# A selective scan with two states on 64 partitions each, and a residual added on TensorE

## What is computed

```python
xz = jnp.einsum('bld,ed->ble', seq, in_proj_w)            # u and z, 256 channels each
u = silu(conv(u) + conv_b)
dt, Bm, Cm = jnp.split(einsum(u, x_proj_w), [8, 24], axis=-1)
dt = softplus(einsum(dt, dt_proj_w) + dt_proj_b)
def step(h, inputs):                                      # 256 channels x 16 states
    h = jnp.exp(dt_t[:, :, None] * A) * h + (dt_t * u_t)[:, :, None] * B_t[:, None, :]
    y = jnp.einsum('bdn,bn->bd', h, C_t)
y = (y + u * D) * silu(z)
x = x + einsum(y, out_proj_w)
t = t + ffn(layernorm(t))
```

## Time and profile before

| | us |
|---|---|
| median of 3 runs | 1285.89 |
| lowest, highest | 1283.64, 1287.6 |
| the profiled execution, its time | 1284.42 |
| its span in the trace | 1282.6 |
| DVE busy in it | 1150.1 |
| POOL busy in it | 1106.9 |
| PE busy in it | 1072.5 |
| ACT busy in it | 819.0 |

### The profile page before, as it was taken

The page is one execution under the profiler, slowest core; times in us unless marked ns, Lnnn a source line. Parts: engine busy times, 40 slices in busy tenths (PEclk is TensorE's granted clock), DMA queues, the critical chain, the costliest instruction groups (busy, mean ns, idle before and its releaser), DMA issues.

```text
span 1282.6 us, 13041 instructions
## 1 busy us (share of the span) xinstructions
PE 1072.5 (84%) x3642; PEld 613.6 (48%) x3642; DVE 1150.1 (90%) x1341; ACT 819.0 (64%) x1532; POOL 1106.9 (86%) x747
## 2 busy tenths in 40 slices
PE   5678878888888887888888889888878878888797
PEld 4334545545545544544455455445445445454344
DVE  1299999999999999999999999999999999999782
ACT  2476766766666667757667666666667676576543
POOL 4199898898898898998988988988988989989663
PEclk8699998998998999999999989989999999998898
DMA  6222221221222312212222212222122132222561
GB/s 162 76 76 76 81 100 65 98 100 58 99 76 86 101 57 105 100 57 98 87 77 80 101 57 99 93 71 99 59 102 101 57 105 100 74 99 87 181 206 37
DMA packets 64538, 116.78 MB, mean 91 GB/s; under 512 B 34218, under 2 KB 47954, under 8 KB 64466
## 3 DMA queue, kind: packets, MB, share of 16 engines
q1 hardware_dynamic: 64466, 115.96, 26.9%
HBM read 108.47 MB, written 7.47 MB: 90 GB/s over the span
## 4 chain that ended last, share of the span: by engine, by line
POOL 27%; DVE 24%; issue 21%; PE 19%; ACT 7%; POOLq 0%; DMA 0%; DVEq 0%; SPq 0%; ACTq 0%
POOL SCAN L414 15%; DVE SCAN L984 15%; PE Yp L711 7%; POOL SCAN L426 6%; DVE SCAN L939 5%; PE PP L740 2%; PE PP L862 2%; PE PP L790 2%; PE PP L842 2%; POOL XN L451 2%; PE PP L835 1%; DVE GATES L968 1%; ACT SGZ L599 1%; POOL GATES L419 1%; POOL XN L442 1%
## 5 line engine op out<-in xcount | busy, mean ns | idle before, releaser
L984 DVE TENSOR_TENSOR_SCAN SCAN<-DA,CAR,SCAN 128x384 f32<-128x384 f32 x768 | 729.8, 1000 | 39.3 <-POOL SCAN L426 35.7
L414 POOL TENSOR_TENSOR SCAN<-SCAN,CS 128x768 f32<-128x768 f32 x384 | 692.3, 1817 | 23.1 <-DVE SCAN L984 18.9
L711 PE MATMUL Yp<-SCAN,IDENT 128*128 128x384 f32 x1536 | 592.6, 511 | 101.1 <-POOL SCAN L414 93.0
L491 ACT ACTIVATE DA<-UDT,A 128x384 f32<-128x384 f32 x768 | 441.6, 581 | 365.3 <-DVE SCAN L984 362.5
L711 PEld LDWEIGHTS Yp<-SCAN,IDENT 128*128 128x128 f32 x1536 | 288.8, 198 | 309.8 <-POOL SCAN L414 147.3
L939 DVE TENSOR_TENSOR SCAN<-UDT,BB 128x768 f32<-128x768 f32 x288 | 268.4, 932 | 11.1 <-PE BB L693 9.2
L426 POOL TENSOR_TENSOR SCAN<-UDT,BS 128x768 f32<-128x768 f32 x96 | 174.4, 1817 | 0.0
L862 PE MATMUL PP<-XN,WT 128*128 128x384 f32 x384 | 140.4, 501 | 0.0
L446 POOL TENSOR_TENSOR UDT<-UDT 128x768 f32<-128x768 f32 x24 | 43.5, 1811 | 69.9 <-DVE UDT L1068 69.9
L862 PEld LDWEIGHTS PP<-XN,WT 128*128 128x128 f32 x384 | 75.6, 199 | 56.7 <-issue 11.7
L693 PE MATMUL BB<-PT,SEL 96*128 96x384 bf16 x288 | 97.7, 340 | 4.1 <-DVE SCAN L939 4.1
(11 more groups left out here) (167 smaller groups left out, 1090.2 us busy)
## 6 DMA issues: line engine op xcount, KB each, us to landing
CS<-bc_rows SPq DMA_DIRECT2D x96, 768.0 KB, 4.1
BS<-bc_rows SPq DMA_DIRECT2D x24, 768.0 KB, 6.0
out<-XN SPq DMA_DIRECT2D x32, 192.0 KB, 2.5
X<-in_x SPq DMA_DIRECT2D x24, 192.0 KB, 3.5
X<-in_L_ffn_memory_tokens SPq DMA_DIRECT2D x16, 256.0 KB, 3.0
XN<-in_L_ffn_memory_tokens SPq DMA_DIRECT2D x16, 256.0 KB, 3.3
bc_rows<-XDT SPq DMA_DIRECT2D x24, 48.0 KB, 1.5
...
```

The lines of the kernel that those rows point to most:

```text
L414: pool.tensor_tensor(M[:, n1 % MRING], HB[:, n1 % HRING], over_halves(CS[:, n1 % CRING]), ALU.mult).then_inc(m_ready, 1)
L491: act.activation(DA[:, h, 0:T], DT[:, par, h], ACT.Exp, scale=A[:, h, n:n + 1])\
L711: last = pe.matmul(Yp[:, h, 0:T], IDENT[:, :], M[:, n3 % MRING, h], start=n3 == 0, stop=n3 == NS - 1)
L984: dve.tensor_tensor_scan(HB[:, s % HRING, h], DA[:, h, 0:T], HB[:, s % HRING, h], CAR[:, ds(J * NS * HALVES + s * HALVES + h, 1)], ALU.mul ...
```

## The change

A step s now handles state s // 2 on partitions 0 to 63 and state 8 + s // 2 on partitions 64 to 127, for half s % 2 of the channels, 64 channels to a free-dimension slot. For this dt and dt u are copied by four DMAs a unit from DTN (DT and DTU, now single) to the double-buffered D4, each 64 partitions to 64 partitions with 4 pieces of 1536 bytes a partition (`spread_dt`). ACT's first decay and DVE's first drive of a unit, and POOL's drives, wait for `d4_loaded`. A selector product serves two steps, so eight of them a unit take the place of twelve, into one bank of BB; it is issued after the Y product of its step. CS and BS are each loaded by two DMAs of 64 partitions. Y is summed by a 128x64 matrix STK (two stacked identities) into the lower or the upper 64 partitions of Yp, by a tile position.

The residual is accumulated in PSUM by an identity product with x, after the projection, which is issued in four pieces of 192 columns; ACT copies the sum to x at step 5. DVE's two adds go. The LESS corrections and the x projection get a bank XP of their own. Softplus moves two steps earlier: dt's product on PE from step 7 to 5, ACT's parts from 8, 9, 10, 12 to 6, 7, 8, 10, POOL's from 11 to 9, DVE's from 13 to 11, and dt times u on POOL from 13 to 12. The carry of the start token is set at step 15 of the unit before the first, by eight short steps, from TDU4, loaded by four small DMAs. Parts left out below are renamed operands of these kinds.

```diff
-HRING, MRING, CRING = 8, 4, 8
+HRING, MRING, CRING = 8, 4, 4
 LAG = 3
 GRP = 4
 GROUPS = NS // GRP
 XROW0 = 64
+HP = P // 2
+PAIRS = NS // 2
...
-        UDT = sb("UDT", [P, 6 * HALVES * T])
-        UDTv = UDT[:, :].rearrange("p (k r h t) -> p k r h t", k=3, r=2, h=HALVES)
-        U, DT, DTU = (UDTv[:, k] for k in range(3))
+        U = sb("U", [P, 2 * HALVES * T])[:, :].rearrange("p (r h t) -> p r h t", r=2, h=HALVES)
+        DTN = sb("DTN", [P, 2 * HALVES * T])
+        DT, DTU = (DTN[:, k * HALVES * T:(k + 1) * HALVES * T].rearrange("p (h t) -> p h t", h=HALVES)
+                   for k in range(2))
+        D4 = sb("D4", [P, 8 * HALVES * T])[:, :].rearrange("p (r k h g t) -> p r k h g t", r=2, k=2, h=HALVES, g=2)
...
-        BB = ctx.enter_context(nc.psum_tensor("BB", [P, 2, 512], F32))
+        BB = ctx.enter_context(nc.psum_tensor("BB", [P, 512], F32))
+        XP = ctx.enter_context(nc.psum_tensor("XP", [P, 512], F32))
...
-                rows = ROWS_D[p, NS + gi * GRP:NS + gi * GRP + GRP]
-                sp.dma_start(CS[:, (gi % 2) * GRP:(gi % 2) * GRP + GRP],
-                             rows.unsqueeze(0).broadcast_to([P, GRP, T])).then_inc(c_loaded[gi % 2], 16)
+                for i in range(2):
+                    rows = ROWS_D[p, NS + i * PAIRS + 2 * gi:NS + i * PAIRS + 2 * gi + 2]
+                    sp.dma_start(CS[i * HP:(i + 1) * HP, (gi % 2) * 2:(gi % 2) * 2 + 2],
+                                 rows.unsqueeze(0).broadcast_to([HP, 2, T])).then_inc(c_loaded[gi % 2], 16)
...
+            def spread_dt(f, p):
+                sp.wait_ge(dtu_ready, f + 1)
+                positive(sp, scan_done, 2 * NS * (f - 1))
+                for g in range(2):
+                    for i in range(2):
+                        sp.dma_start(D4[i * HP:(i + 1) * HP, p, :, :, g].rearrange("p k h t -> p (k h) t"),
+                                     DTN[g * HP:(g + 1) * HP, :].rearrange("p (c t) -> p c t", t=T))\
+                            .then_inc(d4_loaded, 16)
...
+                    spread_dt(J + 1, 1 - par)
                     load_b(J + 1, 1 - par)
                     load_c(J + 1, 1 - par, 0)
...
+            spread_dt(0, 0)
+            sp.wait_ge(set_dve, 10)
+            for g in range(2):
+                for i in range(2):
+                    sp.dma_start(TDU4[i * HP:(i + 1) * HP, g:2 * HALVES:2], TDU[g * HP:(g + 1) * HP],
+                                 allow_slow_non_contiguous=True).then_inc(tdu4_loaded, 16)
...
-                                       over_halves(CS[:, n1 % CRING]), ALU.mult).then_inc(m_ready, 1)
+                                       over_halves(CS[:, n1 // 2 % CRING]), ALU.mult).then_inc(m_ready, 1)
...
-                    pool.tensor_tensor(HB[:, n2 % HRING], DTU[:, par], over_halves(BS[:, pool_index(n2)]),
+                    pool.tensor_tensor(HB[:, n2 % HRING], D4[:, par, 1, n2 % 2], over_halves(BS[:, pool_index(n2)]),
                                        ALU.mult).then_inc(dbu_pool, 1)
-                if front and s == 11:
+                if front and s == 9:
...
+                if front and s == 12:
+                    pool.wait_ge(dt_ready, f + 1)
+                    positive(pool, d4_loaded, 64 * f)
+                    pool.tensor_tensor(DTU, DT, U[:, fp], ALU.mult).then_inc(dtu_ready, 1)
...
-                if front and s == 13:
-                    pool.wait_ge(dt_ready, f + 1)
-                    pool.tensor_tensor(DTU[:, fp], DT[:, fp], U[:, fp], ALU.mult).then_inc(dtu_ready, 1)
...
-                act.activation(DA[:, h, 0:T], DT[:, par, h], ACT.Exp, scale=A[:, h, n:n + 1])\
+                act.activation(DA[:, h, 0:T], D4[:, par, 0, n % 2, h], ACT.Exp,
+                               scale=A[:, n % 2 * 2 + h, n // 2:n // 2 + 1])\
                     .then_inc(da_ready, 1)
...
+                if back and s == 5:
+                    act.wait_ge(op_ready, k + 1)
+                    act.activation(unit_x(k).rearrange("p q t -> p (q t)"), PP[:, 0, 0:T], ACT.Copy).then_inc(x2_ready, 1)
...
-                if front and s == 12:
+                if front and s == 10:
...
-                            act.wait_ge(dt_ready, unit + 1)
+                            act.wait_ge(d4_loaded, 64 * (unit + 1))
...
-                if front and s == 8:
+                if front and s == 6:
...
-            def spread_b(unit, par, n):
-                before = NDVE * unit + dve_index(n)
-                positive(pe, dbu_dve, before - 1)
-                pe.matmul(BB[:, dve_index(n) % 2, 0:T], SEL[:, n], PT[:, par], start=True, stop=True)\
-                    .then_inc(b_ready, 1)
+            def spread_b(unit, par, pair):
+                positive(pe, dbu_dve, NDVE * unit + dve_index(2 * pair))
+                pe.matmul(BB[:, 0:T], SEL[:, pair], PT[:, par], start=True, stop=True).then_inc(b_ready, 1)
             def step(J, par, s, main, front, back, prev, conv, norm):
                 f, k, g, N = J + 1, J - 1, J + 3, NS * J + s
                 fp = kp = 1 - par
-                if main:
-                    if s + 2 < NS and s + 2 not in POOL_STATES:
-                        spread_b(J, par, s + 2)
-                    elif s + 2 >= NS and front:
-                        spread_b(J + 1, 1 - par, s + 2 - NS)
                 if main and s >= LAG or prev and s < LAG:
                     n3 = (s - LAG) % NS
                     pe.wait_ge(m_ready, N - LAG + 1)
                     if s == LAG:
                         positive(pe, v_ready, J)
-                    for h in range(HALVES):
-                        last = pe.matmul(Yp[:, h, 0:T], IDENT[:, :], M[:, n3 % MRING, h],
-                                         start=n3 == 0, stop=n3 == NS - 1)
+                    for c in range(2):
+                        last = pe.matmul(Yp[c * HP:(c + 1) * HP, n3 % 2, 0:T], STK[:, :], M[:, n3 % MRING, c],
+                                         start=n3 < 2, stop=n3 >= NS - 2, tile_position=(0, c * HP))
                     last.then_inc(ysum_done, 1)
+                if main and s % 2 == 0:
+                    if s + 2 < NS:
+                        spread_b(J, par, s // 2 + 1)
+                    elif front:
+                        spread_b(J + 1, 1 - par, 0)
...
-                        last = pe.matmul(PP[:, 0, 0:T], OPT[:, h], VV[:, h], start=h == 0, stop=h == 1)
-                    last.then_inc(op_ready, 1)
+                    for r1 in range(2):
+                        for h in range(HALVES):
+                            pe.matmul(PP[:, 0, r1 * 2 * TOK:(r1 + 1) * 2 * TOK], OPT[:, h],
+                                      VV[:, h].rearrange("p (h r w s) -> p r s h w", h=ROWS, r=2, w=WW)[:, r1],
+                                      start=r1 == 0 and h == 0, stop=False, skip_group_check=True)
+                    pe.matmul(PP[:, 0, 0:T], IDENT[:, :], unit_x(k).rearrange("p q t -> p (q t)"),
+                              start=False, stop=True, skip_group_check=True).then_inc(op_ready, 1)
...
-                if front and s == 7:
+                if front and s == 5:
...
-                        if h == 1:
-                            pe.wait_ge(parts_ready, f + 1)
...
-                dve.wait_ge(b_ready, NDVE * unit + dve_index(n) + 1)
-                dve.tensor_tensor(HB[:, n % HRING], DTU[:, par], over_halves(BB[:, dve_index(n) % 2, 0:T]), ALU.mult)\
+                dve.wait_ge(b_ready, PAIRS * unit + n // 2 + 1)
+                dve.tensor_tensor(HB[:, n % HRING], D4[:, par, 1, n % 2], over_halves(BB[:, 0:T]), ALU.mult)\
...
-                        dve.wait_ge(dtu_ready, J + 2)
+                        dve.wait_ge(d4_loaded, 64 * (J + 2))
...
+                if at(J, -1) and s == 15:
+                    dve.wait_ge(tdu4_loaded, 64)
+                    for i in range(2):
+                        for c in range(2 * HALVES):
+                            last = dve.tensor_scalar(
+                                CAR[i * HP:(i + 1) * HP, c:NS * HALVES:2 * HALVES],
+                                DA[i * HP:(i + 1) * HP, 0, 16 + i * PAIRS:16 + (i + 1) * PAIRS],
+                                TDU4[i * HP:(i + 1) * HP, c:c + 1], None, ALU.mult)
...
-                if back and s == 5:
-                    dve.wait_ge(op_ready, k + 1)
-                    for r1 in range(2):
-                        xr = by_row_parity(unit_x(k), r1)
-                        last = dve.tensor_tensor(xr, xr, seq_rows(PP[:, 0, 0:T], r1), ALU.add)
-                    last.then_inc(x2_ready, 1)
-                if front and s == 13:
+                if front and s == 11:
```

82 lines of the change are left out of this document (43 added, 39 removed).

## The result

| | us |
|---|---|
| before, median of the runs beside the changed kernel's | 1286.09 |
| changed kernel, median of 4 runs | 1427.3 |
| lowest, highest | 1426.36, 1430.27 |
| ratio, 95% interval | 1.1104, 1.108 to 1.1128 |
| span of its profiled execution | 1424.6 |

The change costs 11%. The direction was right; the size was not: 1366 was forecast, and the measured time lies 7 us above the end of the range of 1280 to 1420.

What follows compares the result with a forecast made beforehand. VectorE was taken as the bound. Per unit -1.2 (TensorE) - 0.4 (softplus) + 4.7 (copy) = +3.1 us, over 23 handovers +71, plus 11 at the start: 1366 us, range 1280 to 1420.

Steps and rivals of the forecast that it cites:

- What bounds the kernel: VectorE sets the pace, busy 47.6 of 49.67 us a unit, mostly scans; its only repeated idle time is for POOL's drives.
- the margin of 0.7 us: At the handover the next unit's first drive finds dt times u ready 0.7 us early; the change spends this.
- Part 1: Softplus moved earlier: dt times u ends 5.5 us after scan 11 (t0), VectorE's path grows 1.7 us, L968 saves 0.4.
- Part 2: Copies of dt and dt times u land 9.2 us after issue, one after the other: 4.7 us lost a unit.
- the upper bound of 12 us: Slowest copy landing considered: four half-width copies in sequence at 2.7 us each, plus 1.2 us.
- Part 3: Residual: VectorE loses 0.66 us of adds, but ScalarE's copy delays decay 6 about 0.5 us; hardly a gain by itself.
- Part 4: TensorE's order: 0.0 a unit without overlap of Y pairs, -1.9 us with full overlap; the middle, -1.2, was taken.
- Part 5: Start costs 11 us once: the copy's 9.2 and an estimated 2 for small DMAs and CAR steps; the end costs nothing.
- A: Rival: copies serialize and Y pairs don't overlap, +4.3 us a unit, about 1394 us; chance 0.18.
- B: Rival: the copy's halves fill side by side, pairs at 3/4, +0.1 us a unit, about 1293 us; chance 0.17.
- C: Faster rival: copy takes 5.2 us, pairs overlap, only 0.7 us lost, -1.6 a unit, about 1254 us; chance 0.15.
- the signs named for a wrong forecast: Last copy landing within 6 us, drive 8 waiting over 2 us for the selector, or ScalarE releasing scans 6 to 9.

Runs made afterwards that it cites:

- experiment 4: Changed kernel with POOL's product of dt and u placed ahead of its M product and clamp in step 12: 1386.19 us, ratio 1.0788.
- experiment 2: Changed kernel with as many copies, bytes and pieces, each from 128 to 128 partitions, regrouping left out, only its time counting: 1364.46 us, ratio 1.0619.
- experiment 3: Kernel before with only the residual moved: identity product, ScalarE's copy to x, no adds on VectorE: 1285.74 us against 1285.84, ratio 1.0001.
- the last kernel of 11: Split copy, idle-filling TensorE products, next unit's selector product behind Y at step 14, residual adds back on VectorE: 1317.19 us; with the identity product 1317.31.
- the kernels of 9: Split copy with selector products moved earlier on TensorE, residual adds back on VectorE: 1324.26 us, against 1337.38 with the identity product.
- experiment 10: Idle-filling TensorE products added to the changed kernel alone: 1423.99 us; to the split-copy kernel with earlier selector products: 1352.07, or 1353.22 with adds on VectorE.
- Experiment 11: Split copy, idle-filling products, next unit's selector product behind Y at step 14: 1317.31 us; without the fillers 1325.64; with adds on VectorE 1317.19.

## Why the prediction was wrong

**What bounds the kernel, the margin of 0.7 us, the handover as the place of the loss:** right. VectorE stands there in all 23 handovers, and no other wait costs it more in sum.

**Part 1, when dt times u ends:** right. t0 + 5.8 against 5.5, and the mechanism as written: POOL goes first, and L1103 and the clamp take 2.38 and 1.54 us. One term was off: POOL's M product took 2.44 us where 1.81 stood, so it pays too. That this order of POOL's is a cost in itself is shown by experiment 4 (41 us). The 0.4 us of the softplus step L968 came as 0.5 in the changed kernel (2364 to 1879 ns), but it wasn't a saving that stays: it depends on when POOL is caught up. The Trainium skill ("SBUF — State Buffer", SBUF: two separate sides) says that a VectorE operation with two SBUF inputs and a GpSimd one that reads SBUF exclude each other for a whole instruction, and that the one that starts first has it; the traces agree (958 ns with POOL waiting, 3140 ns in the mean beside POOL, for the two softplus steps of this kind).

**Part 2, the copy:** the mechanism was right and its size too small. I took 197 GB/s for a half-width copy and got 186; that is 0.5 us for 1.57 MB. The rest of the miss is, by the bytes in the windows, the sharing with the loads behind it, for which my sum had no term, since it let the copies go through the queue in order. At 186 GB/s alone they would have landed some 9.6 us after issue (an estimate: 1573 KB, and 1.1 us to the first bytes). The landing was 11.0 and not 9.2 us after issue, so 16.9 - 10.0 = 6.9 us were lost in the handover shown in place of 4.7, and 6.1 in the mean, whose wait is 0.8 us shorter (4.74 for 5.54). The Trainium skill ("SBUF — State Buffer", Door 1) gives about 218 GB/s for 64 partitions; this copy ran at 186, so the estimate of 7.2 us from the page's figure was further off than the 8.0 us from the rows. That width is the cause is shown by experiment 2; the upper bound of 12 us had held it.

**Part 3, the residual:** "hardly a gain by itself" is what experiment 3 shows, and the last kernel of 11 with it. In the kernels of 9, at low clock, it costs 13 us.

**Part 4, TensorE and ScalarE, -1.2 us a unit: this step failed.** The units got 5.46 us longer, 6.1 by the copy and 0.5 less by the softplus step, so about 0.1 is what this part won, where 1.2 was booked. The miss in a unit, 5.5 against 3.1 us, is this 1.1 and the 1.4 us by which the copy was priced too low, less 0.1 of softplus. The pairs do overlap, and fully: the changed kernel's Y product takes 0.87 us where that of the earlier trace rows took 1.45. But the stretch that counts runs at half clock: the granted clock is 0.50 from 736.5 to 742. The timeline of TensorE after the gate product of VectorE:

```profile
736.54 1.55 PE L742 MATMUL Yp<-SCAN,STK 128*64 128x384 f32 x4 [3.69 <-DVE VV L988]
738.37 2.89 PE L776 MATMUL XP<-U,XPT 128*104 128x384 f32 x4 [0.27 <-DVE U L1011]
741.18 1.55 PE L742 MATMUL Yp<-SCAN,STK 128*64 128x384 f32 x4
742.67 0.41 PE L730 MATMUL BB<-PT,SEL 96*128 96x384 bf16 x1
```

The projection of u (L776) takes 2.89 us against 1.71 of L740, two Y products 1.55. The selector product comes at 742.67 and VectorE pays for it:

```profile
743.22 0.95 DVE L977 TENSOR_TENSOR SCAN<-D,BB 128x768 f32<-128x768 f32 x1 [1.26 <-PE BB L730]
744.09 1.92 DVE L1022 TENSOR_TENSOR_SCAN SCAN<-DA,CAR,SCAN 128x384 f32<-128x384 f32 x2
746.60 1.93 DVE L1022 TENSOR_TENSOR_SCAN SCAN<-DA,CAR,SCAN 128x384 f32<-128x384 f32 x2 [0.59 <-ACT DA L524]
749.10 0.95 DVE L977 TENSOR_TENSOR SCAN<-D,BB 128x768 f32<-128x768 f32 x1 [0.57 <-PE BB L730]
```

The prediction looked at drive 8 (the last line, 0.57 us); the larger wait is at drive 6 (1.26), behind the projection of u and two Y products at half clock, and scan 6 waits for its decay (0.59). That is 2.4 us in this unit, while the three waits for POOL (1.8) and the adds (0.66) are gone: together nothing, as the prediction's own count without overlap had it. It had named the clock and then only counted it against the best case. It had also named the single BB bank and given it no cost, and that is where TensorE idles most: the 248.5 us of experiment 10. The faster products leave it idle too (it is busy 62 us less), and the runs don't part the two. So what kept the gain away is shown as waits at half clock; how much of it the one bank is to blame for stays open. Experiment 11 gives the fillers' lift of the clock a price once the copy is out of the way and the order suits it, some 10 us; experiment 10 shows no gain from it in the changed kernel, where the softplus step takes the time back.

**Part 5, the start:** +8.4 where 11 stood, and +2.0 in the first unit. "The end: nothing" was wrong: the end costs 11.4 us like for like, and 10.6 with fillers and split copy. The timeline of VectorE there, of before and of after:

```profile
1213.82 0.96 DVE L950 TENSOR_TENSOR VV<-Yp,GZ 128x768 f32<-128x768 f32 x1 [7.68 <-PE Yp L711]
```
```profile
1355.36 0.96 DVE L988 TENSOR_TENSOR VV<-Yp,GZ 128x768 f32<-128x768 f32 x1 [12.56 <-PE Yp L742]
...
1397.93 3.92 DVE L1022 TENSOR_TENSOR_SCAN SCAN<-DA,CAR,SCAN 128x384 f32<-128x384 f32 x4 [7.06 <-ACT DA L524]
```

VectorE waits 4.9 us longer for Y there. The Y product stands in TensorE's order behind the products on the memory tokens (L830), and these wait for a load:

```profile
PE PP L830 <- DMA X<-in_L_ffn_memory_tokens: 6.9, 1, 6.9
```

SP issues this load at 1332.89, behind the last copy (1321.57), BS and CS; in the kernel before it went out at 1186.43, ahead of the last handover. So the copy has a hand in the end too, by its place in SP's order. The last handover adds 3.0 us (1.62 of wait, 1.42 in L1103), and three short routing steps (L1084 to L1088) take 2.9 us beside POOL where they took 0.5. The 7.06 us for a decay are no new cost of that size: VectorE had waited 5.21 us for a selector product at that place. No run took the end apart.

**The rivals.** A (the pairs don't overlap, 1394) failed by its reason, though its sum was the nearest. B and C needed the halves to fill side by side; the rate of 186 GB/s and the landing of 11.0 us exclude them. Of the signs named for a wrong forecast, one came in part: ScalarE does release scan 6 in the unit shown (0.59 us); it has 28.2 us of VectorE's waits over the kernel. The range reached to 1420 with a copy of 12 us; it left out a TensorE part that wins nothing and a cost at the end.

The sum with the measured terms: 6.1 - 0.5 - 0.1 = 5.5 a unit, x22 = 120; start +8.4, first unit +2.0, end +11.4: 142.
